# State-space scan of a graph network on one core: one program over four groups instead of two, D times x moved to TensorE, gate applied to the accumulator

## The reference, cut to what matters

```python
xc = jax.nn.silu(conv(xc))                      # 256 channels
dbc = xc @ x_proj_w.T                           # 16 columns for dt, 16 for B, 16 for C
dt = jax.nn.softplus(dbc[:, :16] @ dt_proj_w.T + dt_proj_b)
dA = jnp.exp(dt[:, :, None] * A)                # nodes x channels x 16 states
dBx = (dt * xc)[:, :, None] * Bm[:, None, :]
def step(h, t):
    h = dA_t * h + dBx_t
    return (h, h @ C_t)
y = y + xc * D_param
y = y * jax.nn.silu(z)
return y @ out_proj_w.T
```

## Time and profile before

| | |
|---|---|
| median of 3 runs | 7617.66 us (7611.27 to 7618.0) |
| the profiled execution, its own time | 7593.99 us |
| its span, first to last instruction | 7592.3 us |
| mean granted TensorE clock | 0.774 of full |
| the two scan phases | 2507 to 2909 us from the span's start |
| output phase `mamo` | 2909 to 2979 us |
| busy over the whole span | PE 59%, DVE 53%, ACT 24%, POOL 31% |

### The profile page before, as it was taken

The page is one execution under the profiler, slowest core; times in us unless marked ns, Lnnn a source line. Parts: engine busy times, 40 slices in busy tenths (PEclk is TensorE's granted clock), DMA queues, the critical chain, the costliest instruction groups (busy, mean ns, idle before and its releaser), DMA issues. The chain is left out here.

```text
span 7592.3 us, 88522 instructions
## 1 busy us (share of the span) xinstructions
PE 4466.2 (59%) x19132; PEld 2331.9 (31%) x19133; DVE 3997.3 (53%) x6221; ACT 1808.3 (24%) x2757; POOL 2364.8 (31%) x2280
## 2 busy tenths in 40 slices
PE   4887575209992463759556776566774444430583
PEld 2453474103441222635223333223332122220121
DVE  8976474999995894245222332222331111228995
ACT  1574011107872322334001111001110000010352
POOL 0000000400000452000566665666665666630000
PEclk8998687659995776979667887678886666665897
DMA  1471674426662674145555556555665444453443
GB/s 41 160 241 41 222 250 141 154 66 202 180 169 96 222 262 171 59 144 207 163 165 171 187 190 183 157 166 180 195 194 146 135 137 139 138 135 119 139 135 107
DMA packets 505240, 1197.38 MB, mean 158 GB/s; under 512 B 66602, under 2 KB 289653, under 8 KB 492498
## 3 DMA queue, kind: packets, MB, share of 16 engines
q1 hardware_dynamic: 330558, 586.57, 23.9%
q0 software_dynamic: 141200, 464.73, 20.8%
q10 hardware_dynamic: 33396, 145.09, 5.3%
HBM read 924.69 MB, written 274.66 MB: 158 GB/s over the span
## 5 line engine op out<-in xcount | busy, mean ns | idle before, releaser
L2607 POOL DMA_INDIRECT rel1s_rows<-rel_table,rel1s_at x672 | 650.6, 968 | 402.1 <-issue 340.1
L2607 POOL DMA_INDIRECT rel0s_rows<-rel_table,rel0s_at x672 | 652.2, 971 | 380.9 <-issue 346.0
L2607 POOL DMA_INDIRECT rel2s_rows<-rel_table,rel2s_at x672 | 645.5, 961 | 368.9 <-issue 328.9
L2739 PE MATMUL rel2s_acc<-rel2s_rows,rel2s_hot 128*128 x764 | 410.7, 550 | 470.2 <-issue 413.6
L2126 POOL TENSOR_TENSOR mamb_st<-mam_u,mamb_bc 128x1600 f32<-128x1600 f32 x64 | 228.3, 3567 | 1143.3 <-DMA mamb_bc<-dbc 1143.3
L1677 PE MATMUL gatx_acc<-gatx_w,gatx_feat 128*65 128x400 f32 x1600 | 541.0, 501 | 25.1 <-DVE gatx_w L1569 25.1
L2739 PE MATMUL rel0s_acc<-rel0s_rows,rel0s_hot 128*128 x764 | 348.6, 472 | 306.7 <-issue 252.7
L2739 PE MATMUL rel1s_acc<-rel1s_rows,rel1s_hot 128*128 x764 | 341.8, 464 | 293.1 <-issue 230.2
L1569 DVE SCALAR_TENSOR_TENSOR gatx_w<-gatx_w,gatx_adj 128x1600 f32<-128x1600 f32 x200 | 363.3, 1817 | 0.5 <-ACT gatx_w L1625 0.5
L1416 DVE CUSTOM_DVE_ANT_0 gatm_junk<-gatm_srow,gatm_gone 128x3200 bf16<-128x3200 f32 x100 | 343.5, 3489 | 33.5 <-DMA gatm_srow<-gat_scores 29.1
L1677 PE MATMUL latx_acc<-latx_w,latx_feat 128*65 128x400 f32 x800 | 291.9, 509 | 100.6 <-DVE latx_w L1569 100.6
(11 more groups left out here) (611 smaller groups left out, 9572.2 us busy)
## 6 DMA issues: line engine op xcount, KB each, us to landing
mamb_bc<-dbc SPq DMA_DIRECT2D x128, 800.0 KB, 5.8
agg_strip<-strips SPq DMA_DIRECT2D x100, 800.0 KB, 5.8
gatx_adj<-adj SPq DMA_DIRECT2D x200, 400.0 KB, 3.1
adj<-adj_counts SPq DMA_DIRECT2D x25, 1600.0 KB, 7.1
latx_adj<-adj SPq DMA_DIRECT2D x100, 400.0 KB, 3.1
rel_table<-rel0p_prod POOLq DMA_DIRECT2D x25, 1536.0 KB, 6.2
rel_table<-rel0s_prod ACTq DMA_DIRECT2D x25, 1536.0 KB
rel_table<-rel1s_prod ACTq DMA_DIRECT2D x25, 1536.0 KB
```

The lines of the kernel that those rows point to most:

```text
L2607: pool.indirect_dma_start(rows[:, u, k, :], None, table, bass.IndirectOffsetOnAxis(ap=at[:, n:n + 1], axis=0)).then_inc(s_in[u], 16)
L2739: one = nc.tensor.matmul(acc[a][:, :], to, row[:, 0:2 * D], start=fresh and k == 0, stop=False)
```

## The change

- The two phases become one, `mambs`, with 64 turns in the order (channel tile, half, state). SyncE's loads go on across the groups of 16 turns, with the same ring of four buffers and the same two waits.
- GpSimd has one more wait, from turn 2 on: turn q waits until VectorE's multiplication of turn q-2 is done.
- `silu_z` is loaded by SyncE into a tile `z` behind row C of turn 8.
- `xsT` stays in SBUF to the end; `conv_x` is neither stored nor loaded. VectorE makes two matrices `through`, the identity times D. In place of the products of zeros TensorE starts each group with `through` times `xsT` (float32, four pieces), which leaves D x in `acc`.
- In place of ScalarE's four copies, `finish` has VectorE multiply `acc` (PSUM) by `z` (SBUF) into `yT`. For the first three groups it stands behind the recurrence of the next group's first turn, and TensorE starts the next group after it.
- In `mamo` the loads and VectorE's part are gone, TensorE has four PSUM tiles instead of two, and the store is three: 10, 8 and 7 node tiles, each once its pairs are copied.

```diff
-    xc_dram = nc.dram_tensor("conv_x", (2, P, NP), F32).ap()
...
+        xsT = top.sb("xsT", [P, 2, NP])
...
-                        sp.dma_start(xc_dram.rearrange("k p n -> p k n"), xsT[:, :, :]).then_inc(s_st, 16)
-                        sp.wait_ge(s_st, 16)
...
-            for ct in range(2):
-                with Phase(nc, f"mamb{ct}") as ph:
...
-                    todo = [(half, n) for half in range(2) for n in range(S)]
...
+            with Phase(nc, "mambs") as ph:
...
+                groups = [(ct, half) for ct in range(2) for half in range(2)]
+                todo = [(ct, half, n) for ct, half in groups for n in range(S)]
...
+                        if q == S // 2:
+                            sp.dma_start(z[:, :, :], z_dram.rearrange("k p n -> p k n")).then_inc(s_z, 16)
...
+                        if q >= RS:
+                            pool.wait_ge(s_y, q - RS + 1)
+                        if q >= 2:
+                            pool.wait_ge(s_hc, q - 1)
...
-                        def copied(half):
-                            act.wait_ge(s_y, S * (half + 1))
-                            for a, b in spans:
-                                last = nc.scalar.copy(yT[:, ct, half * HALF + a:half * HALF + b], acc[:, a:b])
-                            last.then_inc(s_copied, 1)
...
+                    for ct in range(2):
+                        nc.vector.tensor_scalar(through[:, ct, :], g.ident[:, :], cols[:, 2, ct:ct + 1], None, ALU.mult).then_inc(s_thr, 1)
+
+                    def finish(k):
+                        ct, half = groups[k]
+                        dve.wait_ge(s_z, 16)
+                        dve.wait_ge(s_y, S * (k + 1))
+                        nc.vector.tensor_tensor(yT[:, ct, when(half)], acc[:, 0:HALF], z[:, ct, when(half)], ALU.mult).then_inc(s_out, 1)
...
+                        if q and n == 0:
+                            finish(q // S - 1)
...
+                    finish(len(groups) - 1)
...
-                                for a, b in spans:
-                                    nc.tensor.matmul(acc[:, a:b], g.zeros[:, 0:P], g.zeros[:, 0:b - a], start=True, stop=False)
...
+                            if q:
+                                pe.wait_ge(s_out, q // S)
                             for a, b in spans:
...
+                                nc.tensor.matmul(acc[:, a:b], through[:, ct, :], xsT[:, ct, half * HALF + a:half * HALF + b], start=True, stop=False)
...
-                mm = [ph.ps(f"mm{k}", [P, BANK]) for k in range(2)]
...
+                mm = [ph.ps(f"mm{k}", [P, BANK]) for k in range(4)]
...
+                stores = [(0, 5), (5, 9), (9, len(pairs))]
...
-                    sp.dma_start(xc[:, :, :], xc_dram.rearrange("k p n -> p k n")).then_inc(s_in, 16)
-                    sp.dma_start(z[:, :, :], z_dram.rearrange("k p n -> p k n")).then_inc(s_in, 16)
-                    sp.wait_ge(s_e, len(pairs))
-                    sp.dma_start(nodes(ym_dram), outv).then_inc(s_st, 16)
...
+                    for first, end in stores:
+                        sp.wait_ge(s_e, end)
+                        a, b = pairs[first][0], pairs[end - 1][-1] + 1
+                        sp.dma_start(nodes(ym_dram)[:, a:b, :], outv[:, a:b, :]).then_inc(s_st, 16)
...
-                        v(nc.vector.scalar_tensor_tensor(yT[:, k, :], xc[:, k, :], cols[:, 2, k:k + 1], yT[:, k, :], ALU.mult, ALU.add))
-                        v(nc.vector.tensor_tensor(yT[:, k, :], yT[:, k, :], z[:, k, :], ALU.mult))
```

More of the change, by code:

```diff
@@ L2047, in mamba @@
                 with Phase(nc, "mamae") as pq:
-                    s_st = pq.sem("st")
                     block = pq.block()
@@ L2173, in mamba @@
-            with Phase(nc, "mamo") as ph:
-                xc = ph.sb("xc", [P, 2, NP])
-                z = u
-                out = dt
-                outv = out[:, :, :].rearrange("p k n -> p (k n)").rearrange("p (t d) -> p t d", d=D)
-                mm = [ph.ps(f"mm{k}", [P, BANK]) for k in range(2)]
-                s_in, s_v, s_r, s_m, s_e, s_st = ph.sems("in", "v", "r", "m", "e", "st")
-                pairs = [range(a, min(a + 2, T)) for a in range(0, T, 2)]
+            with Phase(nc, "mambs") as ph:
+                RB, RS = 4, 3
+                z = ph.sb("z", [P, 2, NP])
+                through = ph.sb("through", [P, 2, P])
+                bc = [ph.sb(f"bc{n}", [P, HALF]) for n in range(RB)]
+                st = [ph.sb(f"st{k}", [P, HALF]) for k in range(RS)]
+                carry = ph.sb("carry", [P, S])
+                acc = ph.ps("acc", [P, 4 * BANK])
+                dA = ph.ps("dA", [P, 4 * BANK])
+                s_z, s_thr, s_dA, s_x, s_h, s_kept, s_hc, s_y, s_out = ph.sems(
+                    "z", "thr", "dA", "x", "h", "kept", "hc", "y", "out")
+                s_bc = ph.sems(*(f"bc{n}" for n in range(RB)))
+                spans = [(a, min(a + BANK, HALF)) for a in range(0, HALF, BANK)]
+                groups = [(ct, half) for ct in range(2) for half in range(2)]
+                todo = [(ct, half, n) for ct, half in groups for n in range(S)]
+                when = lambda half: slice(half * HALF, (half + 1) * HALF)
@@ new lines, in _ @@
+                    for q, (ct, half, n) in enumerate(todo):
+                        r, tile = 2 * q + 1, st[q % RS]
+                        dve.wait_ge(s_x, q + 1)
+                        dve.wait_ge(s_dA, q + 1)
+                        if half:
+                            dve.wait_ge(s_kept, ct * S + n + 1)
+                        nc.vector.tensor_tensor_scan(tile[:, :], dA[:, 0:HALF], tile[:, :], carry[:, n:n + 1] if half else 0.0,
+                                                     ALU.mult, ALU.add).then_inc(s_h, 1)
+                        if q and n == 0:
+                            finish(q // S - 1)
+                        dve.wait_ge(s_h, q + 1)
+                        if not half:
+                            nc.vector.tensor_copy(carry[:, n:n + 1], tile[:, HALF - 1:HALF]).then_inc(s_kept, 1)
+                            dve.wait_ge(s_kept, ct * S + n + 1)
+                        dve.wait_ge(s_bc[r % RB], 16 * (r // RB + 1))
+                        nc.vector.tensor_tensor(tile[:, :], tile[:, :], bc[r % RB][:, :], ALU.mult).then_inc(s_hc, 1)
@@ new lines, in mamba, with _ @@
+            with Phase(nc, "mamo") as ph:
+                out = dt
+                outv = out[:, :, :].rearrange("p k n -> p (k n)").rearrange("p (t d) -> p t d", d=D)
+                mm = [ph.ps(f"mm{k}", [P, BANK]) for k in range(4)]
+                s_m, s_e, s_st = ph.sems("m", "e", "st")
+                pairs = [range(a, min(a + 2, T)) for a in range(0, T, 2)]
+                stores = [(0, 5), (5, 9), (9, len(pairs))]
+                block = ph.block()
+                @block.sync
+                def _(sp):
+                    for first, end in stores:
+                        sp.wait_ge(s_e, end)
+                        a, b = pairs[first][0], pairs[end - 1][-1] + 1
+                        sp.dma_start(nodes(ym_dram)[:, a:b, :], outv[:, a:b, :]).then_inc(s_st, 16)
+                    sp.wait_ge(s_st, 16 * len(stores))
+                @block.tensor
+                def _(pe):
```

109 lines of the change are left out of this document (32 added, 77 removed).

## The result

| | before | changed |
|---|---|---|
| median, us | 7617.83 (4 runs) | 7574.12 (4 runs, 7563.03 to 7582.35) |
| ratio | | 0.9944, 95% interval 0.9926 to 0.9961 |
| profiled execution, its own time | 7593.99 | 7582.35 |
| its span | 7592.3 | 7580.7 |
| the stage, from the scan's first exp to the next stage's first transfer | 2506.9 to 2979.1: 472.1 | 2507.9 to 2937.9: 430.0 |

The kernel is 43.7 us faster by the medians; 41.3 were forecast. The interval leaves anything from 30 to 56 us, so that the whole agrees within 2.4 us is luck; what carries the account is the stage, taken from the trace. The two profiled executions differ by 11.6 us only, yet the stage by 42.1.

A forecast was written before the change was run, and what follows sets the result against it. The loads were taken to bound the scan's turn, through a loop over two turns. Terms -12.7 - 1.0 - 32.5 - 1.0 - 6.7 + 6.3 + 6.3 = -41.3 us from 7617.66 gave 7576.4 us, range 7557 to 7600.

The forecast's parts named there:

- 1 border: Between the channel tiles: the 18.53 us between recurrences shrink to one turn of 5.85, -12.7 us.
- The loop of issue, row, GpSimd and multiplication: In the scan: two turns take 11.48 us, 5.74 each, so the loads bound the turn; VectorE alone needs about 5.5.
- part 2: GpSimd's new wait in the scan: over before its row lands, so 0 us; bounds -28.1 and +4.
- Rival A: In the scan, the wait puts GpSimd under every recurrence and multiplications run bare: -28.1 us, time 7548.3; chance 0.10.
- Part 3: Load of silu_z in mid-scan: delays row B of turn 9, making one turn longer, +6.3 us; bounds 0 and +9.3.
- Part 4: Product with z on VectorE's path, three times inside the scan: 2.1 us each, +6.3 us; bounds 4.2 and 15.
- rival B: TensorE has the lower clock at all three borders, the product waiting 1.3 us each: +8.7 us, time 7585.1; chance 0.10.
- Part 5: ScalarE's copies in the middle of a phase no longer make VectorE wait: -1.0 us.
- Part 6: Output phase: loads and VectorE's instructions before TensorE's first product go, -32.5 us; TensorE's higher clock after less idleness, -1.0.
- Part 7: Output store split in three, so only a last piece of 896 KB lands at the end: -6.7 us; bound -5.1.
- Rival D: Later stages run at another granted clock, whose fall could cost 41 us: no difference, time about 7617; chance 0.05.
- The signs: Listed trace observations: right if, among others, three turns lengthen by 1.5 to 2 us; wrong if other stages move over 10.

The follow-up runs named there:

- The run with B first: Changed kernel with SyncE's queue asking for row B of turn q+2 ahead of row C of turn q+1; 7071.39 us, ratio 0.9897 to the kernel before.
- the repeated run: The changed kernel run again, with nothing edited; 7579.74 us, ratio 0.9933 to the kernel before, stage 431.4 us.
- the runs with zeros: Changed kernel with TensorE's groups started by bf16 products of zeros, leaving D times x out of the output; 7580.19 us, stage 431.6 us.
- `silu_z` early: Changed kernel with silu_z loaded beside the small products before the scan instead of behind row C of turn 8; 7094.79 us, ratio 0.9931.
- the kernel before with the two edits of the loop: Kernel before, with row B asked for ahead of row C and GpSimd waiting for the multiplication of turn q-2; 7605.24 us, ratio 0.9966.

## Why the prediction was right, point by point

The sum of the parts in the profiled pair:

| part | forecast | measured | from |
|---|---|---|---|
| 1 border | -12.7 | -12.7 | 18.53 to a mean turn of 5.855 |
| 2 wait, and 5 ScalarE's copies | 0 and -1.0 | -0.4 | 59 other turns at 5.855 for 5.862 |
| 3 load of silu_z | +6.3 | +6.6 | 12.49 less 5.855 |
| 4 three products | +6.3 | +4.7 | 6.91, 7.02, 8.33 less 5.855 each |
| 6 to the first output product | -32.5 | -32.4 | 34.62 to 2.26, from the last addition |
| 6 TensorE's higher clock | -1.0 | -1.0 | first product to last copy: 24.81 to 23.85 |
| 7 store | -6.7 | -6.8 | 12.61 to 5.80, from the last copy |
| start and last turn | 0 | -0.2 | 7.95 to 7.81 to the first recurrence, 10.16 to 10.13 from the last one to the end of its addition |
| sum | -41.3 | -42.2 | each rounded; the stage, 472.1 to 430.0, gives -42.1 |

- **What bounds the turn.** The loop of issue, row, GpSimd and multiplication was read from two turns of the trace. The run with B first shows it by an edit that changes nothing but the place of an issue in the queue of the changed kernel: turns of 5.44. In the kernel before, the same turns came with both edits together. The prediction has one label wrong: the multiplication that ends at 2544.22, and took 2.43, is that of turn 4, not 5 (C of turn 6 waits for it), which is why the loop from there to 2555.73 spans two turns. Its sum and its part 2 hold as they are.
- **Part 2.** The forecast of nothing held, and for the reason given: in 50 of 64 turns the row landed after the wait was over. Rival A was therefore not what happened, but its price was right in kind: once rows are there, the multiplications run bare and the turns save 0.4 us.
- **Part 3** was right in size and mechanism: one turn longer by 6.6.
- **Part 4** was the term that was off, by 1.6 us. The net 1.4 for a product was too much: two turns with a product that waited for nothing are longer than the mean by 1.06 and 1.17. In the rows of the first border the product starts 0.08 us before the recurrence's row ends and the multiplication 0.07 before the product's, so of its 1.79 only 1.61 add to the turn (2622.70, where that multiplication starts, less the 2621.09 at which it would have without); less the stall of 0.44 that is 1.17, near the 1.06 measured there. The reserve for TensorE running behind the float32 products was not needed; with zeros instead nothing changed. The wait for a slow last addition, 1.3, was met once, as priced. That it was met only once is chance: the repeated run met it at another border, and the runs with zeros and with `silu_z` early waited 2.6 and about as much behind additions of 5.8 us, twice the price that rival B put on it.
- **Part 5** is too small to be told from the turns' own spread, and no run has it alone.
- **Part 6** came out within 0.1 in its large term. The -1.0 for TensorE's clock also agrees, but that is luck. The lengths from first product to last copy run from 22.23 to 23.92 us in the kernels with the new output phase, and the kernel before with the two edits of the loop took 23.63 after 34.39 us of idleness. So the 24.81 of the profiled execution before is not what such idleness always costs, and no run shows that the shorter idleness gave anything back.
- **Part 7.** The price of the store, from a line through two other transfers, came out within 0.1; the last piece landed in 4.0 us.
- **Rival D** named the right worry for the span, but not its cause: what follows the stage differs by 30 us between the two executions, at the same granted clock (0.75 from 3300 to 6700 in both).
- **The signs.** By the prediction's own list, other stages that moved by more than 10 us were a sign of being wrong, and they did move. The sign was badly chosen, since in the runs whose kernel before took 7626 or 7630 us the unchanged part behind the stage takes anything from 4633 to 4654. The border turns were to be longer by 1.5 to 2 us each; they were by 1.1, 1.2 and 2.5. The other signs of being right came as listed.
- The rule of the Trainium skill (VectorE: DVE Perf Modes, the table of the TRN2 errata) that a PSUM source costs VectorE 62 cycles more than an SBUF one is not borne out here: the product of PSUM and SBUF took 1.79 to 1.82 us, the one of two SBUF tiles 1.81 at the least.

## What to carry to other kernels

Where every engine waits little and none is full, add up a loop through two turns: an instruction's length can hold a stall, and a transfer's issue can wait in its queue behind a neighbour's condition. Ask for each transfer as soon as its own buffer is free, in the order in which buffers come free. A wait that keeps GpSimd off VectorE's multiplications of two SBUF tiles is worth nothing while GpSimd is late anyway, and all the more once it is early: the two edits belong together. Before a stage's length is put down to an edit, compare the places that the edit does not touch: here TensorE's clock moved single turns by 1.4 to 2.7 us from run to run.

## What the runs showed of the hardware that was not expected

- GpSimd and VectorE block each other both ways and for whole instructions: VectorE's TENSOR_SCALAR on 128x128, 0.28 us alone, took 3.62 and 3.59 beside GpSimd's products, one behind the other; GpSimd's product took 4.53 instead of 3.56 when it began beside a multiplication. The Trainium skill (SBUF: State Buffer, "Who interferes with whom") says that whichever of two such instructions issues first holds the shared ports for all its length, and the other is blocked; the trace agrees. The recurrence (3.48 to 3.55 us) and the product of PSUM and SBUF (1.79 to 1.82) were not slowed in any run.
- TensorE's additions in the scan take 3.0 to 3.3 or, mostly, 4.4 to 5.8 us from turn to turn, by the granted clock (1.00 at 3.01, 0.51 at 5.78), and which border gets a slow one changes from run to run: with GpSimd's wait in place, the turn of the first border takes 6.91 to 8.42 us, that of the second 7.02 to 9.71.
- Stages that gather rows by GpSimd's transfers repeat to some 25 us in 3000 only: from first to last gather, the three relational sums took 3013 and 3039 us together in the two profiled executions, and 3044 in the changed kernel again. On the occasion when the kernel before took 7144 us they took 2553 in two of the runs (without the wait, and B first), and that is nearly all by which the executions there are shorter, while the stage's length stayed the same (430.2 us without the wait).
